# State-space attention in a decoder: the direct term of two heads as one 128-column product at the head of each sum

## The chip, the cores and the metric

The kernel runs on one core of a Trainium2 chip, as one launch. The metric is the device time of that launch in microseconds (us). Engines are named as the profile names them: PE is the matrix engine, PEld its weight loads, DVE the vector engine, ACT the scalar engine, POOL the general-purpose engine, SP the engine that issues most DMAs. A matrix product in float32 shows as two MATMUL records, each with a weight load (LDWEIGHTS) of its own; where a text below says "record", it means one of these.

## The reference, cut to what matters

The model is a decoder of four layers with attention, cross attention and feed-forward blocks. The change is in the first block, a state-space attention with 32 heads of 64 channels over 8 sequences of 256 tokens:

```python
att = qk * decay * lam_ts                       # per head, 256 x 256, causal
y = jnp.einsum('bhts,bshp->bthp', att, v) + D_res
y = y.reshape(B, T, DIM)
yz = y * jax.nn.silu(z)
```

Here `v` is `x * dt` and `D_res` is `x * D`. The diagonal of `att` (a token with itself, level 0) has another factor than the rest, and needs no exponential. The kernel takes it out of the product: for every token and head one number, `coef`, holds the diagonal weight plus `D`, and the direct term of the output is `x * coef`. The other blocks are not touched by the change.

## The kernel before, in words

The block is one software pipeline, in `layer0_attn` (lines 2514 to 3153). The outer unit is a sequence, called a row here (8 of them); the inner unit is a pair of heads, 16 pairs for a row, 128 pairs in all, numbered g. All engines run over the same list of steps s, one pair for a step, and each engine's program is written out in that order; semaphores join them. Work for the next row (projections, convolution, decays, scans, transposes) is laid into fixed steps of the current row by the table `A_AT`.

What belongs to pair g, in order:

- PE, `picks` (line 2758, for two pairs in even steps): spreads the logarithms of the decay into a bank with 32-row products. DVE, `masked_rows` (L3032): masks them into `ru`.
- PE, `exponents` (L2766), step g: one product with 512 columns. ACT, `exps` (L2835): four exponentials into `ex`. DVE, `attend` (L3043), step g: multiplies `ex` by `qk`; raises the semaphore `att`.
- DVE, `values` (L3002, L3006), every even step, for two pairs: `xs`, the inputs times `coef` (tokens on partitions, 256 channels of four heads), which raises `xs`; and `xw`.
- PE, `across` (L2781), `rises` (L2773): the term of the second half of the tokens that comes from the first half. DVE `across` (L3013) makes `far` of them.
- PE, `values` (L2799, L2802), step g + 2: for each half t of the tokens, the sum of two products in the one bank `y_bank`. It runs right behind `exponents` of pair g + 2. The partitions of the bank are channels: head j of the pair has partitions 64 j to 64 j + 63. The weights are 128 x 64, so the output stands in half of the array's columns. First come the products of both heads with `ex` (L2799), then those of both heads with the identity, which add `xs` turned (L2802).
- DVE, `gated` (L3053, L3054), step g + 2: adds `far` to the bank's second half, multiplies by the gate and writes `yzT`; raises `yz`. There is only one `y_bank`, so PE's `values` of pair g waits until `yz` of pair g - 1 has come.
- PE, `output` (L2734), every fourth step, and the squares on ACT and POOL.

`values` on PE waits for four things: `yz` of the pair before, the transposed inputs taken from their bank (in even pairs), `att`, and `xs`.

Of the kernel before, what the change touches and what calls it, by code (L numbers as in the profile page):

```python
# [19 lines left out]
P = 128  # L20
# [2493 lines left out]
def layer0_attn(c):  # L2514
# [14 lines left out]
    H, HD, DI, KC = 32, 64, 2048, 4  # L2529
# [37 lines left out]
    with ExitStack() as stack:  # L2567
# [34 lines left out]
        xs = [sb(f"xs{i}", [P, TB, T]) for i in range(2)]  # L2602
# [7 lines left out]
        sig = Signals(nc, "L0a_c")  # L2610
# [19 lines left out]
        sig = Signals(nc, "L0a")  # L2630
        with nc.Block() as block:
            rv = Ring(sig, "rv", c.banks[0:2])
            rs = Ring(sig, "rs", c.banks[2:4])
            y_bank = c.banks[4]
# [4 lines left out]
            def taken(eng, key):  # L2639

                eng.wait_ge(emptied_by(key), n_emptied[key])
# [26 lines left out]
            def _(pe):  # L2668
                mm, tp = nc.tensor.matmul, nc.tensor.transpose
# [114 lines left out]
                def values(g):  # L2784

                    r, i = divmod(g, NPH)
                    x = xt[r % 2]
                    if g:
                        pe.wait_ge(sig("yz"), g)
                    if i % 2 == 0:  # L2790
                        taken(pe, ("XT", r, i // 2 + 1))
                    pe.wait_ge(sig("att"), g + 1)
                    pe.wait_ge(sig("xs"), g // 2 + 1)
                    e = ex[g % 3]
                    of = lambda j, t: x[:, t, (2 * i + j) * HD:(2 * i + j + 1) * HD]
                    for t in range(TB):
                        ts = slice(t * P, (t + 1) * P)
                        for j in range(2):
                            mm(y_bank[j * HD:(j + 1) * HD, ts], of(j, t), e[:, j, ts], start=True, stop=False)  # L2799
                        for j in range(2):  # L2800
                            own = g % 2 * P + j * HD
                            last = mm(y_bank[j * HD:(j + 1) * HD, ts], xs[g // 2 % 2][:, t, own:own + HD], c.ident[:], start=False, stop=True)  # L2802
                    last.then_inc(sig("valued"), 1)

                for s in steps:
                    if 0 <= s < PAIRS:
                        exponents(s)
                    if 2 <= s <= PAIRS + 1:
                        values(s - 2)
                    if s % 2 == 0 and 0 <= s + 2 < PAIRS:  # L2810
                        picks(s + 2)
                    for what, rho, n in items_at(s):
                        if what in ("TU", "TN"):
                            turn_rows(what, rho, n)
                        else:
                            {"X": project, "D": decays, "XT": turn, "QK": inner, "Z": gate, "O": output, "SS": squares, "F": across, "E": rises}[what](rho, n)
# [539 lines left out]
```

## Time and profile before

| what | value |
| --- | --- |
| time, median of 3 runs | 3812.48 us (3811.46 to 3816.08) |
| profiled execution, its own time | 3805.71 us |
| its span | 3803.9 us, 55022 instructions |
| PE busy | 2993.7 us (79%), 18517 MATMUL records and 18517 LDWEIGHTS |
| DVE busy | 2362.6 us (62%) |
| ACT busy | 1790.9 us (47%) |
| granted clock of PE, mean over the span | 0.9 |
| first and last MATMUL of `values` | 114.8 us, and 1041.3 us |

The span is the time from the first to the last instruction in the trace; the profiled execution's own time is 1.8 us longer. A busy share says how long an engine had some instruction in work. The start of a PE record is exact to some nanoseconds; its length contains the time in which results still come out, so that records overlap, and the distance from one start to the next tells what a record costs.

### The profile page before, as it was taken

To read this page: it belongs to the slowest core of one execution; us is meant where nothing else is said; L and a number is where in the kernel's file an instruction comes from. 1 tells how busy PE (TensorE), PEld (TensorE's weight loads), DVE (VectorE), ACT (ScalarE), POOL (GpSimd) and SP (SyncE) were. 2 spreads that over 40 slices of the span, in tenths; PEclk is the share of its full clock that TensorE was granted. 3 is DMA by queue.
4 is the path that set the end of the run, shared out by engine and by line. 5 is a ranking of instruction groups with operands and counts; after the bars stand their busy time and mean duration, and the time that the engine had idled before them with its cause. 6 is when DMAs were issued, how large, how long until landed. Compare 5 with 4: busy or idle time off the path is not lost. (4 is left out here: it accounts for less than half of the span.)

```text
span 3803.9 us, 55022 instructions
## 1 busy us (share of the span) xinstructions
PE 2993.7 (79%) x18517; PEld 2140.6 (56%) x18517; DVE 2362.6 (62%) x5278; ACT 1790.9 (47%) x4259; POOL 698.8 (18%) x817
## 2 busy tenths in 40 slices
PE   4889889998978789377687671596799858888697
PEld 3667666676656567255455331444598435555485
DVE  5766777677566423777677768697511485555423
ACT  4666666766532222477577454312333325556221
POOL 0000000000110232155344200000111002334422
PEclk8999999999989799699899895798799979999898
DMA  3101101110100368100000000000397101000476
GB/s 102 45 26 48 42 29 34 40 45 29 34 18 1 134 220 277 35 1 1 25 9 4 26 1 0 3 0 9 138 344 274 52 25 35 24 24 12 151 257 209
DMA packets 109094, 264.76 MB, mean 70 GB/s; under 512 B 16880, under 2 KB 71408, under 8 KB 103824
## 3 DMA queue, kind: packets, MB, share of 16 engines
q1 hardware_dynamic: 93328, 229.00, 18.0%
q0 software_dynamic: 8688, 23.78, 1.7%
q10 hardware_dynamic: 6800, 8.46, 0.7%
q8 instruction: 152, 2.49, 0.3%
q14 instruction: 126, 1.03, 0.1%
HBM read 213.65 MB, written 47.54 MB: 69 GB/s over the span
## 5 line engine op out<-in xcount | busy, mean ns | idle before, releaser
L2977 POOL TENSOR_TENSOR L0a_sum_sq<-L0a_sum_sq,L0a_sq 128x512 f32<-128x512 f32 x56 | 76.8, 1372 | 967.1 <-ACT L0a_sq L2919 967.1
L1296 POOL TENSOR_TENSOR L3x_p<-L3x_p,L3x_rsum 128x512 f32<-128x512 f32 x128 | 133.0, 1040 | 447.6 <-DVE L3x_rsum L1377 447.6
L3023 DVE SCALAR_TENSOR_TENSOR L0a_xf<-L0a_xc,L0a_conv,L0a_xf 128x256 f32<-128x256 f32 x432 | 191.3, 511 | 30.1 <-ACT L0a_xf L2884 28.8
L2835 ACT ACTIVATE L0a_ex<-bank,L0a_nb 128x128 f32<-128x128 f32 x512 | 144.6, 368 | 97.1 <-PE bank L2766 96.5
L3032 DVE TENSOR_TENSOR L0a_ru<-bank,L0a_um 128x512 f32<-128x512 f32 x128 | 88.0, 688 | 150.9 <-PE bank L2758 146.0
L1358 DVE SCALAR_TENSOR_TENSOR L3x_s<-bank,L3x_bias 128x512 f32<-128x512 f32 x128 | 86.4, 681 | 132.9 <-PE bank L1136 132.9
L2686 PE MATMUL bank<-x_feat,L0a_wx 128*128 128x256 f32 x576 | 152.7, 415 | 18.7 <-DMA L0a_wx<-in_L0a_wx 13.0
L1986 PE MATMUL bank<-L2a_half,L2a_diag 128*128 128x512 f32 x328 | 144.1, 601 | 28.4 <-ACT L2a_diag L1969 28.4
L1296 POOL TENSOR_TENSOR L1x_p<-L1x_p,L1x_rsum 128x512 f32<-128x512 f32 x128 | 132.2, 1040 | 135.6 <-DVE L1x_rsum L1377 135.6
L1300 POOL TENSOR_TENSOR L1a_p<-L1a_p,L1a_rsum 128x128 f32<-128x128 f32 (+1 forms) x256 | 123.0, 506 | 135.0 <-DVE L1a_rsum L1377 133.0
L2686 PEld LDWEIGHTS bank<-x_feat,L0a_wx 128*128 128x128 f32 x576 | 113.5, 205 | 47.0 <-DMA L0a_wx<-in_L0a_wx 13.2
L2766 PE MATMUL bank<-L0a_ru,L0a_vm 128*128 128x512 f32 x256 | 131.2, 594 | 0.0
L1250 ACT ACTIVATE L1x_p<-L1x_s,L1x_nmax 128x256 f32<-128x256 f32 x256 | 126.7, 499 | 4.6 <-DVE L1x_nmax L1370 4.4
L2725 PE MATMUL bank<-x_feat,L0a_wz 128*128 128x256 f32 x512 | 120.3, 383 | 7.9 <-DVE L0a_far L3013 4.4
L2734 PE MATMUL bank<-L0a_wout,L0a_yzT 128*128 128x256 f32 x512 | 124.5, 399 | 1.0 <-DVE L0a_yzT L3054 1.0
L1986 PEld LDWEIGHTS bank<-L2a_half,L2a_diag 128*128 128x128 f32 x328 | 62.5, 191 | 108.6 <-issue 76.9
L1250 ACT ACTIVATE L3x_p<-L3x_s,L3x_nmax 128x512 f32<-128x512 f32 x128 | 92.0, 719 | 55.9 <-DVE L3x_nmax L1370 55.7
L246 ACT ACT_TABLE_LOAD x7 | 9.0, 1283 | 227.8 <-PEq L57 227.8
L2871 ACT ACTIVATE L0a_xc<-bank,L0a_bx 128x256 f32<-128x256 f32 x144 | 60.4, 470 | 117.7 <-PE bank L2686 117.7
L1250 ACT ACTIVATE L1a_p<-L1a_s,L1a_nmax 128x128 f32<-128x128 f32 (+1 forms) x256 | 113.0, 446 | 3.5 <-DVE L1a_nmax L1368 3.5
L1147 PE MATMUL bank<-ident,L1x_p 128*128 128x128 f32 x512 | 77.4, 285 | 47.2 <-DVE L1x_pT L1346 37.2
L2734 PEld LDWEIGHTS bank<-L0a_wout,L0a_yzT 128*128 128x128 f32 x512 | 101.9, 202 | 19.0 <-issue 4.7
(731 smaller groups left out, 8217.3 us busy)
## 6 DMA issues: line engine op xcount, KB each, us to landing
L2f_wt<-in_L2f_w SPq DMA_DIRECT2D x23, 2180.0 KB, 9.7
L0f_wt<-in_L0f_w SPq DMA_DIRECT2D x39, 898.0 KB, 6.0
L3f_wt<-in_L3f_w SPq DMA_DIRECT2D x39, 768.0 KB, 5.2
L0a_wx<-in_L0a_wx SPq DMA_DIRECT2D x72, 256.0 KB, 3.2
L0a_wz<-in_L0a_wz SPq DMA_DIRECT2D x32, 512.0 KB, 4.3
context_keys_values<-L2f_zeros ACTq DMA_DIRECT2D x32, 256.0 KB, 5.0
L0f_xs<-rows_by_expert SPq DMA_DIRECT2D x39, 128.5 KB, 3.2
L3f_xs<-rows_by_expert SPq DMA_DIRECT2D x39, 128.5 KB, 2.7
```

Of the source, the lines that this page charges most:

```text
L1250: nc.scalar.activation(p_sb[g % NP][:, at:at + nk], s_sb[g % NSB][:, at:at + nk], ACT.Exp, bias=nmax[r % 2][:, i, e:e + 1], accum_out=rsum ...
L1296: last = nc.gpsimd.tensor_tensor(both, both, rsum[r % 2][:, i, :].unsqueeze(2).to_broadcast([P, S, NK]), ALU.mult)
L1300: last = nc.gpsimd.tensor_tensor(one, one, rsum[r % 2][:, i, e:e + 1].to_broadcast([P, nk]), ALU.mult)
L1358: ins = vec.scalar_tensor_tensor(out=s[:], in0=bank[:, 0:W], scalar=scale, in1=bias[r % 2][:].rearrange("p t s -> p (t s)"), op0=ALU.mult, ...
L1986: last = nc.tensor.matmul((odd_banks(k) if i == 1 else both_banks(k))[q][:], diag[:, k, n, :], moved(i, k, j)[:, q * 4:(q + 1) * 4, :], st ...
L2686: last = mm(bank[:, j * T:(j + 1) * T], wx[q % 3][:, k, j * P:(j + 1) * P], x(k), start=(k == 0), stop=(k == KD - 1))
L2725: last = mm(bank[:, d * T:(d + 1) * T], wz[b % 2][:, k, i * P:(i + 1) * P], x(k), start=(k == 0), stop=(k == KD - 1))
L2734: last = mm(bank[:, t * D:(t + 1) * D], yzT[:, g % NY, t * P:(t + 1) * P], wout[:, g % NPH, :], start=(d == 0), stop=(d == GRP - 1))
L2766: rs.fill(mm(bank[:], vm[:], ru[g % 2][:].rearrange("p j t -> p (j t)"), start=True, stop=True))
L2835: last = a(ex[g % 3][:, j, b * P:(b + 1) * P], bank[:, at:at + P], ACT.Exp, bias=nb[r % 2][:, b, h:h + 1])
L3023: vec.scalar_tensor_tensor(out=xf[q % 4][:, j, :], in0=xc[q % 3][:, j, i:i + T], scalar=conv[:, 2 * p + j, i:i + 1], in1=xf[q % 4][:, j, : ...
L3032: ins = vec.tensor_tensor(ru[g % 2][:], bank[:].rearrange("p (j t) -> p j t", j=2), um[:].unsqueeze(1).to_broadcast([P, 2, T]), ALU.mult)
```

## The change

For each half t of the tokens the direct term of both heads becomes one product, whose weights are 128 columns of `xs` (both heads) and whose output stands on all 128 partitions of `y_bank`. It starts the sum; the two products with `ex`, still one for each head, come behind it and end the sum. The waits for the transposed inputs and for `att` move behind the first of the full-width products; the waits for `yz` and `xs` stay ahead of it. The arithmetic is the same but for the order of the sum.

```diff
                     if g:
                         pe.wait_ge(sig("yz"), g)
-                    if i % 2 == 0:
-                        taken(pe, ("XT", r, i // 2 + 1))
-                    pe.wait_ge(sig("att"), g + 1)
                     pe.wait_ge(sig("xs"), g // 2 + 1)
                     e = ex[g % 3]
                     of = lambda j, t: x[:, t, (2 * i + j) * HD:(2 * i + j + 1) * HD]
                     for t in range(TB):
                         ts = slice(t * P, (t + 1) * P)
+                        mm(y_bank[:, ts], xs[g // 2 % 2][:, t, g % 2 * P:(g % 2 + 1) * P], c.ident[:], start=True, stop=False)
+                        if t == 0 and i % 2 == 0:
+                            taken(pe, ("XT", r, i // 2 + 1))
+                        if t == 0:
+                            pe.wait_ge(sig("att"), g + 1)
                         for j in range(2):
-                            mm(y_bank[j * HD:(j + 1) * HD, ts], of(j, t), e[:, j, ts], start=True, stop=False)
-                        for j in range(2):
-                            own = g % 2 * P + j * HD
-                            last = mm(y_bank[j * HD:(j + 1) * HD, ts], xs[g // 2 % 2][:, t, own:own + HD], c.ident[:], start=False, stop=True)
+                            last = mm(y_bank[j * HD:(j + 1) * HD, ts], of(j, t), e[:, j, ts], start=False, stop=True)
                     last.then_inc(sig("valued"), 1)
```

## Rows read from the trace of the kernel before

**Rows 1.** Busy time by engine in one stretch, under its column heads.

```profile
core 0: us, PE busy (x) PEld busy (x) DVE busy (x) ACT busy (x) POOL busy (x), PEclk, DMA share, GB/s
400.00:500.00 100.00, 94.44 (x608) 71.96 (x606) 71.48 (x150) 64.27 (x148) 8.40 (x6) 1.00 0.15 46
```

**Rows 2.** PE by line, 115 to 1050 us: shape, count | busy, mean ns | idle.

```profile
L2766 PE MATMUL bank<-L0a_ru,L0a_vm 128*128 128x512 f32 x250 | 128.1, 594 | 0.0
L2802 PE MATMUL bank<-ident,L0a_xs 128*64 128x128 f32 x1024 | 103.5, 282 | 0.0
```

**Rows 3.** Waits, total us, times, longest: 115 to 1050, then one row, 478.2 to 601.4.

```profile
PE bank L2799 <- DVE L0a_yzT L3054: 58.7, 25, 6.1
...
PE bank L2799 <- DVE L0a_yzT L3054: 7.7, 3, 5.6
...
DVE L0a_ru L3032 <- PE bank L2758: 17.7, 4, 6.1
```

**Rows 4.** Timeline of PE around the values of pair 54: start, length, line, operands.

```profile
536.64 1.02 PE L2766 MATMUL bank<-L0a_ru,L0a_vm 128*128 128x512 f32 x2
537.59 0.44 PE L2799 MATMUL bank<-L0a_ex,ctx_feat 128*64 128x128 f32 x4
...
538.08 0.39 PE L2799 MATMUL bank<-L0a_ex,ctx_feat 128*64 128x128 f32 x4
538.30 0.39 PE L2802 MATMUL bank<-ident,L0a_xs 128*64 128x128 f32 x4
538.61 1.13 PE L2758 MATMUL bank<-L0a_R,L0a_pick 32*128 32x256 f32 x8
```

**Rows 5.** Timeline: full-width groups behind full-width work, and one behind the values.

```profile
546.90 0.61 PE L2781 MATMUL bank<-L0a_qk,L0a_xw 128*128 128x128 f32 x4
...
558.22 0.71 PE L2781 MATMUL bank<-L0a_qk,L0a_xw 128*128 128x128 f32 x4
...
960.78 1.53 PE L2702 MATMUL bank<-ident,L0a_xf 128*128 128x128 f32 x12
960.88 0.69 DVE L3032 TENSOR_TENSOR L0a_ru<-bank,L0a_um 128x512 f32<-128x512 f32 x1 [6.13 <-PE bank L2758]
...
962.15 1.02 PE L2766 MATMUL bank<-L0a_ru,L0a_vm 128*128 128x512 f32 x2
```

**Rows 6.** Timeline of PE in a later block: full rows, then one row.

```profile
2995.63 1.98 PE L2084 MATMUL bank<-L3a_wqk,x_feat 128*128 128x512 f32 x4
2997.54 1.12 PE L2085 MATMUL bank<-L3a_bqk,L3a_ones 1*128 1x512 f32 x2
```

**Rows 7.** Timeline: from the exponents of pair 52 to its values, and pair 54's `attend`.

```profile
499.28 1.02 PE L2766 MATMUL bank<-L0a_ru,L0a_vm 128*128 128x512 f32 x2
...
507.11 2.36 DVE L3064 SCALAR_TENSOR_TENSOR L0a_sp<-L0a_pre,L0a_sp 128x1024 f32<-128x1024 f32 x2 [1.36 <-ACT L0a_sp L2945]
...
512.57 0.42 DVE L3054 TENSOR_TENSOR L0a_yzT<-bank,L0a_zT 128x256 f32<-128x256 f32 x1
...
513.04 0.70 PE L2799 MATMUL bank<-L0a_ex,ctx_feat 128*64 128x128 f32 x4 [5.62 <-DVE L0a_yzT L3054]
...
526.08 0.68 DVE L3043 TENSOR_TENSOR L0a_ex<-L0a_ex,L0a_qk 128x512 f32<-128x512 f32 x1
```

**Rows 8.** Timeline: PE's other waits in this row, and where a DVE run begins.

```profile
526.21 0.44 PE L2799 MATMUL bank<-L0a_ex,ctx_feat 128*64 128x128 f32 x4 [1.62 <-DVE L0a_yzT L3054]
...
527.91 3.37 PE L2686 MATMUL bank<-x_feat,L0a_wx 128*128 128x256 f32 x8 [0.60 <-DVE L0a_coef L3106]
...
543.02 0.46 DVE L3124 COPY L0a_nb<-bank 128x32 f32<-128x32 f32 x2
...
548.87 0.44 PE L2799 MATMUL bank<-L0a_ex,ctx_feat 128*64 128x128 f32 x4 [0.50 <-DVE L0a_yzT L3054]
...
562.16 1.99 PE L2725 MATMUL bank<-x_feat,L0a_wz 128*128 128x256 f32 x8 [0.61 <-DVE L0a_far L3013]
```

**Rows 9.** Timeline of PE in the last row, behind the values of pair 123.

```profile
1027.33 0.44 PE L2799 MATMUL bank<-L0a_ex,ctx_feat 128*64 128x128 f32 x4 [0.82 <-DVE L0a_yzT L3054]
...
1029.38 0.68 PE L2781 MATMUL bank<-L0a_qk,L0a_xw 128*128 128x128 f32 x4 [0.96 <-DVE L0a_xw L3006]
```

## Prediction, made before the changed kernel ran

> **What bounds the kernel now.** I read the page first, then the busy time by stretches, then PE's lines and waits in the stage that the change touches (115 to 1050 us), and last the timeline of one row. PE is busy 94.44 of 100 us in a stretch of that stage, DVE 71.48 [rows 1]. PE waits before the values 25 times, 58.7 us in all [rows 3], and DVE's longest wait is for PE's picks, 17.7 us in one row [rows 3]. So PE sets the pace of most steps, with a few places in each row where PE waits for DVE. What one added PE nanosecond costs depends on which of these two kinds of place it falls in.
>
> **What the change removes.** For each half of the tokens two 64-column products with the identity (four records) become one full-width product (two records). L2802 goes from 1024 records [rows 2] to half of them. This is no halving of time. A group of four records of L2799 starts at 538.08, the L2802 group at 538.30, so four records cost 0.22 us [rows 4]. A full-width record with the same 128 moving columns costs (0.61 - 0.27) / 3 = 0.11 us from the clean L2781 group, with a record's own length of 0.27 at full clock [rows 5]. Two of these cost 0.22 us. The four narrow records already run as two pairs, one head beside the other in its own half of the columns, so the removed and the added product have the same price: 0.
>
> **What the moved waits give.** `att` of pair 54 is raised by DVE's L3043, which ends at 526.76, and its values start at 537.59 [rows 4, 7]. In DVE's program `attend` of pair g, `values` of pair g's inputs and the use of the transposed inputs all come before `gated` of pair g - 1, and the wait for that one stays in front. So the moved waits never end last: 0. Nothing is newly queued behind them either, since they are met when PE comes to them.
>
> **What the change adds: two more changes of the array's shape per half.** Before, a pair's `values` is entered once from full width and left once. After, full-width and half-width products alternate: full, half, full, half. From `exponents`, which is full width, the first product is now no change of shape; then come half, full, half, and the next item. That is two entries into the half shape and two exits instead of one each: one entry and one exit more for a pair.
>
> The price of each, from starts at full clock:
> - Entry, gap: L2766's last record starts 1.02 - 0.59 = 0.43 behind its first, at 537.07, and the values start at 537.59, 0.52 later, where a 512-column record itself costs 0.43 [rows 2, 4]. Gap 0.09. The wait is met already. In contrast L2702's twelve records end with one that starts at 960.78 + 1.53 - 0.27 = 962.04 and L2766, which also has a semaphore to take (its DVE input was ready at 961.57), starts at 962.15, one record's 0.11 later [rows 5]. No gap without a change of shape.
> - Entry, exposed weight load: the first group of values lasts 0.44, the third 0.39 [rows 4]. 0.05.
> - Exit, gap: the last L2802 group starts at 538.30, four such records cost 0.22, L2758 starts at 538.61 [rows 4]. 0.09.
> - Exit, exposed load: L2781 behind the values lasts 0.71, behind full width 0.61 [rows 5]. 0.10.
>
> Sum 0.09 + 0.05 + 0.09 + 0.10 = 0.33 us; with the hundredths that rounding drops I take 0.34 us for a pair that comes without waiting. If PE waits at the pair's head, the entry gap that used to vanish in the wait comes back inside, and the first load is a long one: 0.10 + 0.14 + 0.19 + 0.14 - 0.05 = 0.52 us.
>
> Is it the shape or the semaphore? All changes next to `values` carry a wait. L2084 to L2085 in a later block have none between them: four 512-column records should cost 4 x 0.43 = 1.72, and the next shape starts 2997.54 - 2995.63 = 1.91 later, 0.19 more, of which 0.10 is the group's own first load and 0.09 the gap [rows 6]. So it is the shape. The Trainium skill has the rule, "TensorEngine Tiling (Array Packing)", Tiling Modes, Key Properties: to change the tiling mode drains the engine, to change tiles within a mode does not. By that rule this change, which halves the instructions, is a loss; the rows agree and give the size that the page doesn't.
>
> **What lies beside other work.** I go along row 3 of the batch (pairs 48 to 63, 478 to 601 us).
> - Pairs 50, 51 (places 2, 3 of the row) come behind `exponents` of pair 52 at 499.28. From there ACT and DVE carry the chain (exponentials, the row's softplus at 507.11, then `gated` at 512.57) until PE starts pair 52 at 513.04, having idled 5.62 [rows 7]. Hidden.
> - Pair 52 itself runs at half clock (0.70 for a group instead of 0.44) and is followed by idle 1.62 ahead of pair 53, behind a DVE scan [rows 7, 8]. Its growth, 2 x 0.34 to 0.52, is hidden.
> - Pair 53: 0.52 against idle 0.60 ahead of L2686, released by a DVE chain that doesn't need the values [rows 8]. Hidden.
> - Pair 54: exposed, 0.34; DVE's next run starts only with L3124 at 543.02, on PE's transposes.
> - Pairs 55, 56, 57: that DVE run lasts from 543.02 to the release of L2725 at 562.16. Pair 55's growth goes into the idle 0.50 ahead of pair 56; pairs 56 and 57 bring 0.52 + 0.34 against 0.61 idle [rows 8]. 0.25 exposed.
> - Pairs 58 to 63 and 48, 49: eight, with no idle time on PE. 8 x 0.34 = 2.72.
>
> A row: 0.34 + 0.25 + 2.72 = 3.31 us. Seven rows: 23.2 us. If the covers were gone altogether, 128 x 0.34 = 43.5 us.
>
> The last row has no work for a next one, and repeats in four steps with idle 0.82 and 0.96 around every fourth pair [rows 9]: that pair's growth is hidden by the 0.96, the one behind it waits first (0.52), two more cost 0.34. Three times 1.20, then 1.9 for the last four pairs, where PE and DVE take turns: 5.5 us.
>
> **Sum.** 23.2 + 5.5 = 28.7 us, on the profiled execution's 3805.7: 3834.4. The median of the runs is 6.8 us above that execution, so I name 3812.5 + 28.7 = 3841. The time at half clock stays where it is: the idle of 5.62 shrinks to some 4.9, and what PE does at half clock behind it is hidden anyway.
>
> **The rivals.**
> - Only the gaps cost, the load is not exposed. The Trainium skill says in "TensorE: Matmul & The Clock Gate", Part 1, on the array's sub-arrays, that a product can begin before its load completes. As a mechanism here: growth 0.09 + 0.09 = 0.18 a pair, and 28.7 x 0.18 / 0.34 = 15 us: 3828. Against it: 0.71 against 0.61, and 0.44 against 0.39 [rows 4, 5]. Chance 0.10.
> - The cover fails: DVE, late by PE's growth, passes it on, all 128 pairs count, with some at 0.52. 43 to 50 us: 3859. Against it: DVE's chains in the hidden places start before the growth. Chance 0.10.
> - DVE is the true pace and PE's growth goes into slack: 0 to 7 us, 3815. Against it: in eight places of a row PE has no idle time, and DVE waits for its picks [rows 3]. Chance 0.05.
> - Faster: the price is not the shape's but that of a first load which must take a semaphore not long met. Then the first full-width load is fetched ahead under `exponents`, which saves 0.14 a pair, and the inner changes cost nothing. Eleven to twelve pairs a row count as above, 28.7 x 0.14 / 0.34 = 12 us less: 3801. It decides from the point where the three inner changes of a pair cost under 0.14 together. For it: every change around `values` has a wait. Against it: rows 5 and 6. Chance 0.04.
>
> **How the numbers follow.** Forecast 0.71, rivals 0.10, 0.10, 0.05, 0.04. The forecast's own range is 3835 to 3848. To leave out no more than 2 in 10 it reaches to the two nearer rivals: 3823 to 3859. A change under 0.2% (7.6 us) can't be told from none; slower than that are the forecast and the first two rivals, 0.91; the third gives same, 0.05, the fourth faster, 0.04.
>
> **What would show it.** MATMUL records fall from 18517 by 512. A pair that comes without waiting takes from `exponents`' last start to the next item 538.61 - 537.07 = 1.54 us now [rows 4] and should take 1.54 + 0.34 = 1.9. The new product's two records start 0.11 apart behind `exponents` and about 0.21 in the second half. The row grows from its 123 us (the stretch of rows 3) by 3.3. The idle ahead of pair 52 shrinks by about 0.7, that ahead of pair 56 nearly vanishes. It would be wrong if the inner gaps were under 0.09, or if the row's length grew by much less than its unhidden pairs.

## The result, and the profile after the change

The changed kernel takes 3846.13 us (median of 5 runs, 3839.10 to 3850.88); the kernel before takes 3816.08 us beside it (5 runs, 3811.46 to 3825.29). The ratio is 1.0077, interval 1.0063 to 1.0091: slower by 0.8%, some 29 us. Forecast was a loss of 28.7 us.

From the page of the kernel after:

```profile
span 3845.6 us, 53998 instructions
PE 3048.4 (79%) x18005; PEld 2167.0 (56%) x18005; DVE 2361.6 (61%) x5278; ACT 1793.2 (47%) x4259; POOL 697.3 (18%) x817
```

There are 512 MATMUL records and as many weight loads fewer, and PE is busy 54.7 us longer than before. DVE, ACT and POOL did the same work in the same time.

The timeline of PE around pair 54, which answers to [rows 4]:

```profile
547.13 1.02 PE L2766 MATMUL bank<-L0a_ru,L0a_vm 128*128 128x512 f32 x2
547.99 0.38 PE L2795 MATMUL bank<-ident,L0a_xs 128*128 128x128 f32 x2
548.30 0.44 PE L2801 MATMUL bank<-L0a_ex,ctx_feat 128*64 128x128 f32 x4
548.67 0.49 PE L2795 MATMUL bank<-ident,L0a_xs 128*128 128x128 f32 x2
549.09 0.44 PE L2801 MATMUL bank<-L0a_ex,ctx_feat 128*64 128x128 f32 x4
549.46 0.91 PE L2758 MATMUL bank<-L0a_R,L0a_pick 32*128 32x256 f32 x5
```

The first full-width product starts 0.86 behind `exponents`' first start, twice a 512-column record's 0.43, so without a gap. Its two records should cost 0.22, but the narrow ones start 0.31 later: 0.09 is the entry gap. Each narrow group lasts 0.44, not 0.39 (the load, 0.05), and is left 0.37 after its start, where 0.22 + 0.05 would do: the exit gap, 0.10. The second full-width group lasts 0.49 instead of 0.38, its exposed load. From `exponents`' last start, 547.13 + 0.43 = 547.56, to the picks it is 1.90 us; before it was 1.54 [rows 4], and the prediction said 1.9.

PE's waits before the values, whole stage (115 to 1085 us), and then those of row 3 (487.8 to 614.1 us):

```profile
PE bank L2795 <- DVE L0a_yzT L3053: 52.3, 19, 5.7
...
PE bank L2795 <- DVE L0a_yzT L3053: 7.1, 2, 5.3
PE bank L2725 <- DVE L0a_ss L3136: 0.6, 1, 0.6
PE bank L2773 <- DVE L0a_yacc L3130: 0.2, 1, 0.2
```

The waits before the values shrink from 58.7 in 25 to 52.3 in 19 [rows 3]. In row 3 the wait ahead of pair 56, the one ahead of L2725 for `far`, and that ahead of L2686 for `coef` [rows 8] are gone: PE's growth has filled them.

```profile
523.53 0.80 PE L2795 MATMUL bank<-ident,L0a_xs 128*128 128x128 f32 x2 [5.26 <-DVE L0a_yzT L3053]
536.71 0.49 PE L2795 MATMUL bank<-ident,L0a_xs 128*128 128x128 f32 x2 [1.84 <-DVE L0a_yzT L3053]
```

Pairs 52 and 53 started at 513.04 and 526.21 [rows 7, 8]: both are late by the same 10.5 us, although pair 52 itself grew from 1.91 to 2.71 us. What PE does between them costs nothing, as the map said (the prediction's list of the places of a row where PE's growth is hidden or exposed). The idle time ahead of pair 53 didn't shrink for it, but grew from 1.62 to 1.84. The `output` group between the two pairs, first before, then after, tells why:

```profile
518.72 5.01 PE L2734 MATMUL bank<-L0a_wout,L0a_yzT 128*128 128x256 f32 x16
530.01 4.00 PE L2734 MATMUL bank<-L0a_wout,L0a_yzT 128*128 128x256 f32 x16
```

In both kernels the granted clock is at its lower level for some 10 us here (0.50 from 511.3 to 521.5 before, from 520.5 to 530.8 after). Counted from the start of pair 52 that stretch now ends 1.2 us earlier, so more of the group runs at the full clock, which gave back more than the pair had grown.

### The profile page after: what moved, and what is told of

It is laid out like the page before. It is cut to its first block and busy times, and to the rows that moved or that the text cites. A ratio compares the mean times of both kernels' runs of the same rounds, so it can differ in the third digit from the quotient of the medians.

```text
span 3845.6 us, 53998 instructions
## 1 busy us (share of the span) xinstructions
PE 3048.4 (79%) x18005; PEld 2167.0 (56%) x18005; DVE 2361.6 (61%) x5278; ACT 1793.2 (47%) x4259; POOL 697.3 (18%) x817
## 3 DMA queue, kind: packets, MB, share of 16 engines
q14 instruction: 126, 1.03, 0.1%
## 5 line engine op out<-in xcount | busy, mean ns | idle before, releaser
L2795 PEld LDWEIGHTS bank<-ident,L0a_xs 128*128 128x128 f32 x512 | 87.4, 197 | 147.5 <-DVE L0a_yzT L3053 80.6
L2686 PE MATMUL bank<-x_feat,L0a_wx 128*128 128x256 f32 x576 | 153.3, 416 | 15.1 <-DMA L0a_wx<-in_L0a_wx 13.0
L2795 PE MATMUL bank<-ident,L0a_xs 128*128 128x128 f32 x512 | 120.5, 319 | 53.4 <-DVE L0a_yzT L3053 52.3
L2686 PEld LDWEIGHTS bank<-x_feat,L0a_wx 128*128 128x128 f32 x576 | 114.7, 207 | 44.1 <-DMA L0a_wx<-in_L0a_wx 13.2
L2725 PE MATMUL bank<-x_feat,L0a_wz 128*128 128x256 f32 x512 | 118.4, 382 | 3.7 <-DVE L0a_ss L3136 3.5
```

Source lines behind the costliest of these rows:

```text
L2686: last = mm(bank[:, j * T:(j + 1) * T], wx[q % 3][:, k, j * P:(j + 1) * P], x(k), start=(k == 0), stop=(k == KD - 1))
L2725: last = mm(bank[:, d * T:(d + 1) * T], wz[b % 2][:, k, i * P:(i + 1) * P], x(k), start=(k == 0), stop=(k == KD - 1))
L2795: mm(y_bank[:, ts], xs[g // 2 % 2][:, t, g % 2 * P:(g % 2 + 1) * P], c.ident[:], start=True, stop=False)
```

## The experiments

All are timed in five rounds against the kernel before on the same chip. To see the stage alone, I use two DVE instructions that all kernels share: the first scan of row 0 (70.69 us before) and the last scaling of the squares (1047.13 us before), 976.4 us apart. After the change they stand at

```profile
70.20 2.62 DVE L3079 TENSOR_TENSOR_SCAN L0a_gcT<-L0a_ones,L0a_R 128x128 f32<-128x128 f32 x8
...
1076.13 0.16 DVE L3136 TENSOR_SCALAR L0a_ss<-bank 128x2 f32<-128x2 f32 x1 [0.17 <-PE bank L2743]
```

1005.9 us apart, 29.5 more. It helps to split the stage at the first records of the values of pair 0 and of pair 111, the last pair of the seventh row. Pair 111 starts at

```profile
963.11 0.44 PE L2799 MATMUL bank<-L0a_ex,ctx_tok 128*64 128x128 f32 x4
985.28 0.38 PE L2795 MATMUL bank<-ident,L0a_xs 128*128 128x128 f32 x2
```

before and after. Differences to the kernel before, in us:

| run | scan to pair 0 | pair 0 to pair 111 | pair 111 to the end | stage |
| --- | --- | --- | --- | --- |
| the change | 0.56 | 22.10 | 6.83 | 29.5 |
| e1 | 0.59 | 0.84 | 0.00 | 1.4 |
| e2 | 0.05 | 22.29 | 6.63 | 29.0 |
| e3 | -0.11 | 7.35 | 5.47 | 12.7 |
| e4 | 0.83 | -13.56 | -1.69 | -14.4 |
| e5 | 0.66 | 0.04 | 1.25 | 2.0 |
| e6 | 0.16 | 22.72 | 5.58 | 28.5 |
| e7 | 0.30 | -19.54 | -2.93 | -22.2 |

No values run in the first part, so its differences of up to 0.8 us don't come from them. Each row of the table is a single execution.

**e1: the change's order, narrow products.**

```diff
-    mm(y_bank[:, ts], xs[..., g % 2 * P:(g % 2 + 1) * P], c.ident[:], start=True, stop=False)
+    for j in range(2):
+        mm(y_bank[j * HD:(j + 1) * HD, ts], xs[..., own:own + HD], c.ident[:], start=True, stop=False)
```

> The order and the waits of the change, but the direct term stays two products of 64 columns for each half of the tokens, put first in the sum. Theory A (the array's shape: each entry into and exit from the half-width shape costs PE a gap of 0.09 us and an exposed load of 0.05 to 0.10) : no added change of shape, so the time of the kernel before, ratio 0.999 to 1.001, and a pair without waiting takes 1.02 us from its first record to the next item, as before. Rival B (the new order or the new place of the waits costs something): most of the +29 us of the change is here too, ratio near 1.007.

Measured: 1.0001 (0.9985 to 1.0017); stage +1.4 us. So the order of the sum and the place of the waits cost nothing, and rival B falls. Of the 1.4 us, 0.6 lie ahead of pair 0, and 0.8 came in one step between pairs 53 and 54; neither repeats from row to row.

**e2: the change with its waits at the head.**

```diff
+    if i % 2 == 0:
+        taken(pe, ("XT", r, i // 2 + 1))
+    pe.wait_ge(sig("att"), g + 1)
     pe.wait_ge(sig("xs"), g // 2 + 1)
     ...
-        (both waits behind the first product)
```

> The change with all four waits ahead of the first product, as in the kernel before; only the full-width product and its place are kept. Theory A: the time of the change, ratio 1.007 to 1.009 against the kernel before, 1.47 us from a pair's first record to the next item, inner gaps of 0.09 although no semaphore is taken inside. Rival B (a load that must take a semaphore is what costs): the gaps inside the pair vanish and the ratio falls to 1.002 or under.

Measured: 1.0073 (1.0052 to 1.0094); stage +29.0 us. Pair 54, with no semaphore to take inside:

```profile
546.57 0.38 PE L2798 MATMUL bank<-ident,L0a_xs 128*128 128x128 f32 x2
546.88 0.44 PE L2800 MATMUL bank<-L0a_ex,ctx_feat 128*64 128x128 f32 x4
547.25 0.49 PE L2798 MATMUL bank<-ident,L0a_xs 128*128 128x128 f32 x2
547.67 0.44 PE L2800 MATMUL bank<-L0a_ex,ctx_feat 128*64 128x128 f32 x4
548.04 0.70 PE L2758 MATMUL bank<-L0a_R,L0a_pick 32*128 32x256 f32 x4
```

The distances are those of the change to the hundredth: 0.31, 0.37, 0.42, 0.37. The gaps belong to the shapes.

**e3: full, narrow, narrow, full.**

```diff
+    wide(0, start=True, stop=False);   near(0, 0); near(0, 1)
+    near(1, 0, start=True); near(1, 1, start=True);   last = wide(1, start=False, stop=True)
```

Here `wide(t)` is the full-width direct product of half t, `near(t, j)` the product with `ex` of head j.

> Both direct terms at full width, but the first half of the tokens as full, narrow and the second as narrow, full: one entry and one exit for a pair, as before, with the change's full-width products. Theory A: where a full-width item follows (odd steps) the pair costs the same as before to 0.02 us; in even steps the picks with 32 rows follow, and one more change of shape, 0.19 us, comes in. So half of the pairs cost 0.2 more, 28.7 x 0.10 / 0.34 = 8 us over the kernel before, ratio 1.002. Rival C (the full-width product itself costs more than the four narrow records it replaces): as slow as the change, ratio 1.007.

Measured: 1.0025 (1.0011 to 1.0039); stage +12.7 us.

```profile
539.68 1.02 PE L2766 MATMUL bank<-L0a_ru,L0a_vm 128*128 128x512 f32 x2
540.54 0.39 PE L2798 MATMUL bank<-ident,L0a_xs 128*128 128x128 f32 x2
540.85 0.66 PE L2800 MATMUL bank<-L0a_ex,ctx_feat 128*64 128x128 f32 x8
541.44 0.49 PE L2798 MATMUL bank<-ident,L0a_xs 128*128 128x128 f32 x2
541.86 1.13 PE L2758 MATMUL bank<-L0a_R,L0a_pick 32*128 32x256 f32 x8
```

The same full-width products with fewer changes of shape cost less than half of the change's loss, so it isn't their own price (rival C falls). From `exponents`' last start, 540.11, to the picks it is 1.75 us, 0.21 over the kernel before: the picks bring the one more change. The sum came out at 12.7 us instead of 8. In the first seven rows it was 7.4 us; the last row and the stage's end gave 5.5. Of that 2.1 is the last `output` group, 5.75 us where it lasted 3.69 before, and some 0.7 the values of the last pair, inside which the clock fell to its lower level:

```profile
1050.15 1.07 PE L2800 MATMUL bank<-L0a_ex,ctx_feat 128*64 128x128 f32 x8
```

against 0.66 for the same group of pair 54. For the remaining 2.7 I had scaled down the change's own share, which gave 1.6, instead of counting that row anew.

**e4: the other products in two halves of 64 columns.**

```diff
+    def mh(out, weights, moving, **k):
+        if not halves[0]:
+            return mm(out, weights, moving, **k)
+        for h in range(2):
+            last = mm(out[h * HD:(h + 1) * HD], weights[:, h * HD:(h + 1) * HD], moving, **k)
+        return last
```

`mh` takes the place of `mm` in all of PE's products of the stage but the values, the picks and the transposes; `halves[0]` is set in steps 0 to 129, and for the items only where the step has no transposes or is odd.

> The kernel before, with PE's other products of the stage (exponents, projections, decays, gates, outputs, across, rises, squares) written as two products of 64 columns side by side, except in the even steps that hold transposes. So exponents, values and the items of most steps share one shape. Theory A: in a row 11 entries and 8 exits go; those in places where PE sets the pace are 9 entries (0.14 each) and 5 exits (0.19 each), 2.2 us, 15.5 us for seven rows and 2 to 3 us in the last: 18 us faster, ratio 0.995. If the halves don't run side by side at 256 and 512 moving columns, it is slower by 100 us and more. Rival B: no change of time.

Measured: 3793.28 us against 3815.17, ratio 0.994 (0.9916 to 0.9964); stage -14.4 us. This kernel beats both. Pair 55, an odd step:

```profile
536.14 1.08 PE L2676 MATMUL bank<-L0a_ru,L0a_vm 128*64 128x512 f32 x4
537.05 0.39 PE L2807 MATMUL bank<-L0a_ex,ctx_feat 128*64 128x128 f32 x4
537.27 0.39 PE L2810 MATMUL bank<-ident,L0a_xs 128*64 128x128 f32 x4
537.49 0.39 PE L2807 MATMUL bank<-L0a_ex,ctx_feat 128*64 128x128 f32 x4
537.71 0.39 PE L2810 MATMUL bank<-ident,L0a_xs 128*64 128x128 f32 x4
537.93 1.90 PE L2676 MATMUL bank<-x_feat,L0a_wx 128*64 128x256 f32 x16
```

There are twice the records in the same time: 16 records of 256 columns last 1.90, and 8 full-width ones behind full-width work 1.89 (L2725 at 494.97 us of the kernel before). All four groups of the values follow at 0.22, the next item too: neither gap nor exposed load. The gain in seven rows was 13.6 us (forecast 15.5), that of the last row 1.7 (forecast 2 to 3).

**e5 and e6: the change in some places only.** `i` is the pair's place in its row.

```diff
+    if i in (2, 3, 4, 5, 7):        # e6: i not in (2, 3, 4, 5, 7)
+        (full width first, as in the change)
+    else:
+        (as before)
```

> The change's order (full-width product first in each half) only in the places 2, 3, 4, 5 and 7 of each row of 16 pairs, 40 of 128 pairs; the others as before. By the map of the prediction PE's growth there runs beside DVE and ACT: nothing in seven rows, and 0.34 + 0.52 + 0.34 = 1.2 us in the last, ratio 1.000. Rival (each added PE time counts wherever it stands): 40 x 0.35 = 14 us, ratio 1.0037.

> The change's order only in the other places, 0, 1, 6 and 8 to 15, 88 of 128 pairs. By the map nearly the whole of the change's loss is here: 3.3 us a row, 23 for seven, 4 to 5 in the last: 27 to 28 us, ratio 1.007. Rival (each added PE time counts wherever it stands, and the rest is DVE's): 88/128 of 29, 20 us, ratio 1.005.

Measured: e5 1.0008 (0.9996 to 1.0021), stage +2.0 us; e6 1.0075 (1.0055 to 1.0096), stage +28.5 us. The lines of PE in the stage (115 to 1085 us), first e5, then e6, show how many records each has at full width (columns as in [rows 2]):

```profile
L2799 PE MATMUL bank<-ident,L0a_xs 128*64 128x128 f32 x704 | 68.4, 273 | 0.0
L2798 PE MATMUL bank<-ident,L0a_xs 128*128 128x128 f32 x160 | 41.7, 347 | 46.8 <-DVE L0a_yzT L3062 46.6
```

```profile
L2798 PE MATMUL bank<-ident,L0a_xs 128*128 128x128 f32 x350 | 77.8, 304 | 5.8 <-DVE L0a_yzT L3062 5.6
L2799 PE MATMUL bank<-ident,L0a_xs 128*64 128x128 f32 x320 | 36.6, 313 | 0.0
```

Forty pairs with the same growth on PE cost 2.0 us, the other 88 cost 28.5: the same edit, priced by its place. The change's 29.5 us shared out by number would have been 9 and 20. In e5 the 35 pairs of the first seven rows cost nothing (0.04), the five of the last row 1.25, where 1.2 was forecast; the other 0.7 lie ahead of pair 0.

**e7: no direct term.** The kernel before without the products of `xs` with the identity; the direct term is missing from its output.

> Leaves out the direct term altogether (the products of xs with the identity); xs is still made and waited for. Four slots of 0.11 us a pair go, and no change of shape. Theory A with the same map: 0.44 us in the nine to ten open places of a row, 4.2 us, 29 for seven rows, 4 in the last: 33 us faster, ratio 0.991, the same size as the change's loss, so that the change's two more entries and exits cost nearly as much as the whole direct term. If DVE takes over the pace as soon as PE is faster, half of that, ratio 0.996.

Measured: 3791.34 us, ratio 0.9945 (0.9928 to 0.9963); stage -22.2 us. PE's part is as expected:

```profile
526.80 0.59 PE L2766 MATMUL bank<-L0a_ru,L0a_vm 128*128 128x512 f32 x1
527.33 0.66 PE L2800 MATMUL bank<-L0a_ex,ctx_feat 128*64 128x128 f32 x8
527.91 1.13 PE L2758 MATMUL bank<-L0a_R,L0a_pick 32*128 32x256 f32 x8
```

The values take 0.58 instead of 1.02, 0.44 less. But a third of the forecast gain was missing, since DVE took over part of the pace (PE's waits from 115 to 1050 us):

```profile
PE bank L2800 <- DVE L0a_yzT L3055: 71.8, 26, 6.6
PE bank L2781 <- DVE L0a_xw L3007: 14.6, 19, 1.8
PE bank L2686 <- DVE L0a_coef L3107: 6.3, 7, 1.0
PE bank L2725 <- DVE L0a_far L3014: 5.6, 8, 0.8
```

PE waits longer in each of these places (71.8 where it was 58.7 [rows 3]). The map held for a growth of PE; for this gain it gave an upper bound. On PE the whole direct term is 0.44 us a pair, and the entry and exit that the change adds are 0.35: nearly as much as the work that it rearranges.

## Why the prediction was right, point by point

- **Removed against added products: 0.** Right. e3 and e4 show the price by columns: four narrow records, side by side in twos, cost what two full ones do.
- **Moved waits: 0.** Right: e1 and e2 differ from their partners by nothing that can be measured.
- **An entry and an exit more a pair, 0.34 us.** Right: 1.90 - 1.54 = 0.36 with rounding, and e2 shows that no semaphore has a part in it. Nor has the bank in which both shapes sum: the same gap stands between `exponents` and the values, which write different banks, and in e1 the narrow products follow each other in that one bank with no gap. (The change halves the records of the direct term, not those of the values, as the prediction's wording could be read: these go from 16 to 12 a pair.) For pairs that wait at their head I had 0.52. Pair 56, which waits before and after, measured 0.55: from its first record to the picks 561.28 - 559.71 = 1.57 us, against 549.89 - 548.87 = 1.02 before.
- **The map.** 3.31 us a row were forecast. Pair 111 starts at 985.28 instead of 963.11; pair 0 started 0.07 late. That is 22.1 us for seven rows, forecast 23.2: from the first pair of a row to that of the next 3.20 to 3.22 in six rows, and 2.95 in the seventh. The missing 0.1 a row: I had left 0.25 exposed for pairs 56 and 57, and the idle time there swallowed nearly all of it. e5 and e6 show the map by themselves. Two details of it were off and cost nothing. The idle time ahead of pair 52 shrank by 0.36 (5.62 to 5.26), not by 0.7: pair 51's growth went into another wait, which the prediction doesn't name,

```profile
505.89 0.68 PE L2781 MATMUL bank<-L0a_qk,L0a_xw 128*128 128x128 f32 x4 [0.37 <-DVE L0a_xw L3006]
```

  and which is gone after the change. And the stretch at half clock did not stay where it was: it covers more of the idle time ahead of pair 52 and ends earlier behind it, and in row 3 the next one begins inside pair 53. From its start to L2686 that pair takes 2.06 us instead of 1.10 without the idle time, more than the 0.60 of idle that was to hide it; yet the next `exponents`, at 547.13 instead of 536.64 [rows 4], is late by the same 10.5 us, behind PE's wait of 0.2 for DVE's L3130.
- **The last row, 5.5 us.** Too small with the stage's end, which gave 6.8 us together; 0.6 more of the 29.5 lie ahead of pair 0. Without what follows the row gave 5.1, and it went on growing by 0.35 a pair that doesn't wait, as said. What I didn't have is in the `output` group behind the last pair. Before and after:

```profile
1042.54 3.69 PE L2734 MATMUL bank<-L0a_wout,L0a_yzT 128*128 128x256 f32 x16 [0.95 <-DVE L0a_yzT L3054]
1069.86 5.38 PE L2734 MATMUL bank<-L0a_wout,L0a_yzT 128*128 128x256 f32 x16 [0.95 <-DVE L0a_yzT L3053]
```

  In the stretch 1062 to 1075 us the granted clock is 0.87, while it was 1.00 from 1036 to 1046 before: PE had idled 0.28, 0.86 and 0.95 between the last pairs, before as after, but the fall to the lower of the two levels (1.2 GHz) now came inside the group and not behind it. 1.7 us. In e2, e3 and e6, where the last pairs have full-width products of `xs` too, the group lasts 5.17 to 5.75; in e1, e4 and e5, where they have none, 3.69. But in e7, which has no product of `xs` at all, it lasts 5.36 as well: so the full-width products are not needed for it. What these groups share is the time of the fall, just ahead of the group or inside it.
- **The time.** 29.5 in the stage against 28.7. That the sum came so close is in part luck: the seven rows and the last gave 1.5 us less than forecast, and the 1.7 us of the clock and the 0.6 ahead of pair 0, which no term had, made up for it. The absolute number, 3841, was 5 us under the measured 3846, mostly because the median of the kernel before moved from 3812.5 (its first three runs) to 3816 (all five).
- **Not from the change.** The profiled execution after is 41.7 us longer in its span than that of before, more than the runs show. 12.7 us of it lie behind the stage, in blocks that the change doesn't touch. From the end of the stage to the end of the span the kernel before takes 2756.8 us, and the other eight kernels 2756.7 to 2770.9, though all have the same program there. After the change, some 9.5 us of it arise in the feed-forward block of layer 2, between two DVE instructions (L761 and a later L842) that are 64.6 us apart before and 74.1 after; in e2, which has the change's products and order, they are 65.8 apart, in e6 74.3. The trace shows where, here PE before, PE after, and ACT's wait after:

```profile
2769.26 3.74 PE L432 MATMUL bank<-L2f_xsT,L2f_wt 128*128 128x128 f32 x32
2806.12 6.08 PE L432 MATMUL bank<-L2f_xsT,L2f_wt 128*128 128x128 f32 x32 [5.02 <-ACT L2f_zeros L582]
ACT L2f_zeros L582 <- DMA context_keys_values<-L2f_zeros: 10.1, 1, 10.1
```

  ACT waited 10.1 us for a DMA to land, PE 5.0 us for ACT, and the group behind it ran in part at the lower clock. Before, PE had no such wait there, and the granted clock was 1.00 from 2764.9 to 2776.5 us, where it is 0.82 in the same work after (2796.5 to 2815.7). It is a difference between single executions; why the DMA came late in these two was not tried.

The first rival (only the gaps cost, 15 us) fell to the group lengths 0.49 against 0.38 and 0.44 against 0.39. The second (all pairs count, 43 to 50 us) fell to e5, the third (PE's growth goes into slack) to e6. The fourth (faster) fell to e2.

## What to carry to other kernels

Count the changes of the array's shape, not the instructions: a run of products keeps its shape for free, and each entry into or exit from half-width work cost 0.14 to 0.20 us of PE here. Where products of both shapes alternate, write the wide ones as halves side by side and the stage has one shape; that gained 0.6%, where the opposite lost 0.8%. And price an edit by the place in which its engine sets the pace: the same 0.35 us a pair cost nothing in the 35 pairs of seven rows that e5 changed, and all of itself in most of the 88 pairs of e6.

## What the runs showed of the hardware

- Products split into two halves of 64 columns kept the full rate at 128, 256 and 512 moving columns (8 records 0.60 to 0.61, 16 records 1.90, 4 records 1.03), although PE has twice the instructions; I had given that a doubt in the expectation of e4.
- The gap at a change of shape didn't depend on a semaphore (the change and e2 have the same distances), on the direction (0.09 to 0.10 both ways), or on the columns of what came before (128 or 512 moving columns). The exposed load did depend on the direction: 0.05 into the half-width shape, 0.10 to 0.11 out of it.
